# x2 closed by VectorE with its statistics right behind, the gate's halving folded in, two copies of ScalarE moved ahead

## The reference, cut to what matters

```python
h = relu(layernorm(x))
v = h @ W0                                   # 12 heads of 32
a = softmax(mask(leaky(src(tanh(v)) + dst(tanh(v)).T)))
gate = sigmoid(h @ H_w.T + H_b)
x2 = x + gate * elu(a @ v + b) + (1 - gate) * h
h1 = relu(layernorm(x2))
q, k, v1 = h1 @ Wq + bq, h1 @ Wk + bk, h1 @ Wv + bv
out = x2 + softmax(mask(q @ k.T / 8)) @ v1 @ Wf + bf
```

## Time and profile before

| what | value |
| --- | --- |
| timed runs, median of 3 | 1011.37 us (1010.96 to 1014.32) |
| profiled execution, its own time | 1006.25 us |
| its span | 1004.5 us |
| TensorE busy | 926.7 us, 92% |
| VectorE busy | 786.5 us, 78% |
| ScalarE busy | 641.2 us, 64% |
| GpSimd busy | 278.5 us, 28% |
| mean granted TensorE clock | 0.979 of full |

### The profile page before, as it was taken

The page is one execution under the profiler, slowest core; times in us unless marked ns, Lnnn a source line. Parts: engine busy times, 40 slices in busy tenths (PEclk is TensorE's granted clock), DMA queues, the critical chain, the costliest instruction groups (busy, mean ns, idle before and its releaser), DMA issues.

```text
span 1004.5 us, 24765 instructions
## 1 busy us (share of the span) xinstructions
PE 926.7 (92%) x9851; PEld 817.8 (81%) x9851; DVE 786.5 (78%) x1473; ACT 641.2 (64%) x1309; POOL 278.5 (28%) x337
## 2 busy tenths in 40 slices
PE   6599999999999999999999999999999999999595
PEld 5386888988888898888889888888988888898475
DVE  5877777879777787977778797777879777886804
ACT  5647658484865858486585848658584865857242
POOL 2224050331506033150603315060331506032210
PEclk9799999999999999999999999999999999999887
DMA  8303252231526223152522415252241525221102
GB/s 221 66 3 32 34 97 34 71 42 18 97 33 97 33 69 44 19 96 34 97 33 68 45 20 96 33 97 33 69 45 18 96 34 97 33 59 19 20 32 64
DMA packets 185077, 56.41 MB, mean 56 GB/s; under 512 B 166402, under 2 KB 184964, under 8 KB 184964
## 3 DMA queue, kind: packets, MB, share of 16 engines
q1 hardware_dynamic: 184964, 54.83, 31.2%
HBM read 17.07 MB, written 12.58 MB: 30 GB/s over the span
## 4 chain that ended last, share of the span: by engine, by line
PE 71%; DVE 22%; issue 2%; ACT 1%; SPq 1%; DMA 1%; POOL 0%; ACTq 0%; DVEq 0%; POOLq 0%
PE ps L694 12%; PE ps L696 12%; PE ps L695 12%; PE ps L761 8%; PE ps L765 7%; PE ps L762 7%; PE ps L680 5%; DVE p L1072 4%; DVE mx L1070 3%; DVE p L1044 3%; DVE x L1032 3%; PE ps L774 3%; DVE rs L1040 3%; PE ps L897 3%; PE ps L840 1%
## 5 line engine op out<-in xcount | busy, mean ns | idle before, releaser
L439 POOL TENSOR_TENSOR x_in<-x_in,ee 128x384 f32<-128x384 f32 x64 | 68.5, 1070 | 563.9 <-DVE ee L1057 563.9
L426 POOL TENSOR_TENSOR x_in<-x_in,bf_row 128x384 f32<-128x384 f32 x64 | 84.0, 1342 | 50.6 <-ACT p L459 50.6
L1070 DVE TENSOR_REDUCE mx<-ps 128x6 f32<-128x384 f32 x64 | 35.2, 550 | 75.8 <-PE ps L840 75.8
L1085 DVE COPY_PREDICATED_SCALAR z<-not_adj,masked 128x768 f32 x64 | 69.9, 1092 | 29.4 <-ACT z L550 29.4
L955 DVE TENSOR_TENSOR hT1l<-ps,hT1h 128x384 fp32r<-128x384 f32 x128 | 62.5, 549 | 26.0 <-ACT hT1h L464 26.0
L680 PE MATMUL ps<-ident,p 128*128 128x128 f32 x384 | 54.6, 287 | 26.9 <-DVE p L1044 15.5
L680 PEld LDWEIGHTS ps<-ident,p 128*128 128x128 f32 x384 | 44.6, 146 | 32.6 <-issue 18.3
L513 ACT ACTIVATE ps<-hb_all 128x384 f32<-128x384 f32 x56 | 27.6, 493 | 66.9 <-DVE x_in L1097 66.9
L531 ACT ACTIVATE QT<-ps,bq_col 128x512 f32<-128x512 f32 x48 | 33.0, 688 | 58.4 <-PE ps L765 58.4
L694 PE MATMUL ps<-Wf_hi,hT1h 128*128 128x384 f32 x192 | 67.6, 352 | 1.2 <-DVE x L1032 0.6
L432 POOL TENSOR_TENSOR x_in<-x_in,h 128x384 f32<-128x384 f32 x64 | 64.2, 1035 | 14.4 <-DVE Wf_lo L985 14.4
(11 more groups left out here) (134 smaller groups left out, 2815.7 us busy)
## 6 DMA issues: line engine op xcount, KB each, us to landing
x_in<-in_x_dram SPq DMA_DIRECT2D x16, 768.0 KB, 5.0
V<-v_tok SPq DMA_DIRECT2D x64, 192.0 KB, 5.8
V<-v_tok SPq DMA_DIRECT2D x128, 96.0 KB, 2.4
out_dram<-x_in SPq DMA_DIRECT2D x16, 768.0 KB, 3.5
x<-in_L_gnn_H_w_dram SPq DMA_DIRECT2D x1, 576.0 KB, 6.1
QT<-in_L_gnn_W_dram SPq DMA_DIRECT2D x3, 192.0 KB, 6.9
thT<-in_L_gnn_Wq_dram SPq DMA_DIRECT2D x1, 576.0 KB, 5.5
z<-in_L_gnn_Wk_dram SPq DMA_DIRECT2D x1, 576.0 KB, 6.5
```

Source lines behind the costliest of these rows:

```text
L426: pool.tensor_tensor(x_in[:, j % 3, t], x_in[:, j % 3, t], bf_row[:], ALU.add).then_inc(x2_biased, 1)
L439: pool.tensor_tensor(x_in[:, i % 3, t], x_in[:, i % 3, t], ee[:, t], ALU.subtract).then_inc(x2_made, 1)
L1070: dve.tensor_reduce(mx1[:, q], bank.rearrange("p (h m) -> p h m", m=N), AX_X, ALU.max).then_inc(max1_made, 1)
L1085: dve.copy_predicated(zu, not_adj[:, tiles].unsqueeze(2).broadcast_to((P, 2, PAIRS0, N)), masked0[:].unsqueeze(2).unsqueeze(3).broadcast_t ...
```

## The change

VectorE, in place of GpSimd, makes x2: `close(t)` gets a fourth instruction, x_in = -0.5 * ee + x_in, and the statistics of that tile follow it at once, each waiting for the one before. The gate stays g = tanh(z/2): ScalarE's four instructions that formed (1 + g) / 2 are gone, the third instruction of `close` multiplies by (g + 1), and the halving is the -0.5 of the fourth. The 1 that was added to h - ee goes into the second instruction. ScalarE's copies of the last two blocks of turned probabilities stand ahead of `exp1(2)` and `exp1(3)` now.

```diff
             # GpSimd
-                if real(i):
-                    pool.wait_ge(x_plus_h, TILES * (i + 1))
-                    for t in range(TILES):
-                        pool.wait_ge(gated, TILES * i + t + 1)
-                        pool.tensor_tensor(x_in[:, i % 3, t], x_in[:, i % 3, t], ee[:, t], ALU.subtract).then_inc(x2_made, 1)
             # ScalarE
-                if real(i):
-                    for t in range(TILES):
-                        act.wait_ge(gate_tanh, TILES * i + t + 1)
-                        act.activation(gate[:, t], gate[:, t], ACT.Identity, scale=0.5, bias=half[:]).then_inc(gate_made, 1)
...
-                exp1(2)
-                exp1(3)
                 if real(i):
                     for q in range(4, 6):
                         act.wait_ge(probs0_turned, 6 * i + q + 1)
                         act.activation(thT[:, q - 3], ps[:, job("probs0T_copied", q) % BANKS], ACT.Copy).then_inc(probs0T_copied, 1)
+                exp1(2)
+                exp1(3)
             # VectorE, close(t)
                         dve.wait_ge(elu_made, n)
+                        dve.scalar_tensor_tensor(x1[:, t], h0[:, par, t], 1.0, ee[:, t], ALU.add, ALU.subtract).then_inc(h_less_elu, 1)
+                        dve.wait_ge(h_less_elu, n)
+                        dve.wait_ge(gate_tanh, n)
+                        dve.scalar_tensor_tensor(ee[:, t], gate[:, t], 1.0, x1[:, t], ALU.add, ALU.mult).then_inc(gated, 1)
+                        dve.wait_ge(gated, n)
                         dve.wait_ge(x_plus_h, n)
-                        dve.tensor_tensor(x1[:, t], h0[:, par, t], ee[:, t], ALU.subtract).then_inc(h_less_elu, 1)
-                        dve.wait_ge(h_less_elu, n)
-                        dve.wait_ge(gate_made, n)
-                        dve.scalar_tensor_tensor(ee[:, t], x1[:, t], 1.0, gate[:, t], ALU.add, ALU.mult).then_inc(gated, 1)
-
-                def stats_of_x2(t):
-                    if real(i):
-                        dve.wait_ge(x2_made, TILES * i + t + 1)
+                        dve.scalar_tensor_tensor(x_in[:, i % 3, t], ee[:, t], -0.5, x_in[:, i % 3, t], ALU.mult, ALU.add).then_inc(x2_made, 1)
+                        dve.wait_ge(x2_made, n)
                         row_stats(1, x_in[:, i % 3, t], t, i)
...
                 close(3)
-                stats_of_x2(0)
-                stats_of_x2(1)
                 add_out(2)
                 values0(i + 1, 2)
-                stats_of_x2(2)
-                stats_of_x2(3)
```

## The result

| | before | after |
| --- | --- | --- |
| timed runs, median | 1011.43 us (1010.96 to 1014.32, 4 runs) | 1025.64 us (1024.86 to 1026.73, 4 runs) |
| ratio of the runs, 95% interval | | 1.0135 (1.0114 to 1.0156) |
| profiled execution, span | 1004.5 us | 1023.1 us |
| VectorE busy | 786.5 us | 807.3 us |
| ScalarE busy | 641.2 us | 612.5 us |

The change makes the kernel slower, by 14.2 us in the medians and by 18.6 us in the two profiled spans. The forecast was 17.0 more (1028.4, within 1020 to 1036).

What follows compares the result with a forecast made beforehand. TensorE, busy 92%, was taken to bound the kernel, with VectorE holding it up behind the scores. Stalls of 14.6 us plus 1.4 and 1.0 at the ends made 17.0; 1011.37 + 17.0 = 1028.4 us, range 1020 to 1036.

Steps and rivals of the forecast that it cites:

- The chain of the closing: On VectorE, four distances of 0.59 us plus a 0.465 statistic make a closing 2.825 instead of 1.66.
- What GpSimd's x2 had cost VectorE: Two closing instructions slowed while GpSimd made x2; with GpSimd idle, 0.70 + 0.58 = 1.28 us come back per body.
- The bank: `add_out(2)`, 2.45 us later, frees gate tile 2's bank too late: TensorE stalls 1.04 us in 14 bodies, 14.6 us.
- The slack of 1.54: `add_out(2)` ended at 483.57 and could end as late as 485.11 without delaying TensorE at gate tile 2.
- The other deadlines: Behind the first stall, h1 (slack 0.6 us) is in time by 0.1, and gate tile 3 has no second wait.
- ScalarE: Dropping four halvings, 2.1 us a body, and copying sooner gain nothing: ScalarE waits for TensorE, and VectorE's chain holds behind the scores.
- The rival in which the exponentials come late: Behind the scores, moved copies delay the exponentials, so `divide1(1)` waits in 15 bodies: 7.5 us on top, 1036; chance 0.09.
- The ends: In the first and last group TensorE waits for h1, so later `row_sums` counts directly: +1.4 and +1.0 us.
- The rule on semaphores: Semaphores between chained VectorE instructions cost nothing, so closing distances are 0.48: rival of 1012.4 us, chance 0.06; forecast used 0.59.

Runs made afterwards that it cites:

- the statistics back where they stood: The change with x2's four statistics at their earlier places, two behind the last closing, two behind values0 of tile 2: 1014.35 us, ratio 1.0073.
- `add_out(2)` sooner: The change with `add_out(2)` moved one closing earlier, right behind `add_out(1)`: 1021.58 us against 1008.12, ratio 1.0140.
- The pairs: The change with closings of two tiles interleaved, and `add_out(1)`, `add_out(2)` and the values at other places: 1006.23 us against 1008.24, ratio 0.9979.
- the second comparison: The unedited change timed again beside the kernel before, on another chip than at first: 1025.18 us against 1007.83, ratio 1.0183.
- ScalarE's part alone: The change with x2 by GpSimd again, statistics at their earlier places, halving left out, sooner copies kept: 1008.66 us against 1008.12, ratio 1.0006.
- the pairs with the two moves: Interleaved closings, plus next body's mask at the body's end and `divide0(3)` between attention 1's second and third low parts: 1002.39 us, ratio 0.9940.

## Why the prediction was right

**The chain of the closing.** A closing was foreseen at 2.825 us and measures 2.84. The distance between waiting neighbours was foreseen at 0.59 and measures 0.58 to 0.60 in four places of each closing. The instruction that was not in the trace takes 0.56, with 0.60 to the next. What GpSimd's x2 had cost VectorE went away as foreseen: no closing instruction is over 0.56. The Trainium skill ("SBUF — State Buffer", section "🔬 SBUF: two separate sides") says that VectorE with two SBUF inputs and a GpSimd instruction that reads SBUF take the shared ports as an exclusive lock, each for the whole instruction. The traces here agree. VectorE's long instructions of 1.25 to 1.26 and 1.13 us are there in the kernel before and with x2 by GpSimd again, each has two SBUF inputs and starts while GpSimd's x2 runs, and none is there in the change.

**The bank.** `add_out(2)` was to come 2.45 later and comes 2.50; the stall was to be 1.04 and is 1.07 at the tile and 1.06 in the body (59.67 less 58.61). It stands 14 times among TensorE's waits, as foreseen. The slack of 1.54 is bracketed: 0.90 and 1.09 of delay cost nothing at that tile, 2.50 costs 1.07.

**The other deadlines.** h1 was to be in time by 0.1 in the change, because the first stall delays TensorE too, and no wait for it shows. It does show once the first stall is taken away, in two kernels, and makes the projections about 0.2 us late in each.

The larger part of what those two kernels lose is at gate tile 3: 0.22 of 0.42 us a body, and 0.75 of 0.92. The prediction asked whether tile 3 would wait in the change, and was right that it would not, but it did not read the slack of that bank. Rows of the kernel before give it, on VectorE, ScalarE and TensorE:

```profile
485.15 0.52 DVE L1097 TENSOR_TENSOR x_in<-ps,x_in 128x384 f32<-128x384 f32 x1
...
486.28 0.49 ACT L513 ACTIVATE ps<-hb_all 128x384 f32<-128x384 f32 x1
...
487.26 0.33 PE L694 MATMUL ps<-Hw_hi,hT0h 128*128 128x384 f32 x1
```

`add_out(3)` ends at 485.67 and, by the same reading as for tile 2, could end as late as 486.67 (487.26 - 0.50 - 0.09): a slack of 1.00 us, less than tile 2's. With the statistics back where they stood it comes 1.10 later, with `add_out(2)` sooner 1.60 later, and both wait. In the change it comes 1.58 later, but TensorE is 1.07 late by then, so only 0.51 of the slack is used.

**ScalarE.** Its part is worth nothing, in both kernels that take its parts alone or away, and the reason is the one given: the 0.5 us that TensorE saves it waits for `divide1` later. The rival in which the exponentials come late can be read off the change itself, on ScalarE and VectorE:

```profile
468.32 0.97 ACT L566 ACTIVATE p<-p 128x384 f32<-128x384 f32 x2
...
469.83 0.94 DVE L1031 TENSOR_REDUCE rs<-p 128x12 f32<-128x768 f32 x1
```

The last two exponentials end at 469.29 and `divide1(1)` starts at 469.83: 0.54 us to spare, where 0.5 was foreseen.

**The ends.** The prediction had +1.4 at the first group and +1.0 at the last. TensorE's wait at the turning of h1 in the first group and in the last answers to the earlier trace rows:

```profile
79.08 2.98 PE L671 MATMUL ps<-ident,p 128*128 128x128 f32 x12 [1.29 <-ACT p L454]
...
972.86 2.79 PE L671 MATMUL ps<-ident,p 128*128 128x128 f32 x12 [10.93 <-ACT p L454]
```

The first comes 1.68 later, of which 0.3 was there ahead of the closings (the first of them starts at 63.04 instead of 62.72); the last wait is 10.93 instead of 9.88, 1.05 more.

**The rule on semaphores.** The Trainium skill ("VectorE: DVE Perf Modes", section "The DRAIN you can't avoid") measured eight copies and found that a semaphore after each costs nothing extra. For the instructions of this case a wait for the one right ahead does cost: 0.59 against 0.47 in one and the same operation and shape. The measurement decides. The pairs keep every wait of the change and run at 0.47, so it is not the semaphore as such that costs, but having to wait for the instruction right ahead. What the 0.12 us is made of was not tried. The pairs took the ratio from 1.0183 to 0.9979, about 19 us; `add_out(2)` sooner alone gave 4.

**The size.** The prediction had 17.0 us; the second comparison gives 17.4 and the first 14.2. The terms add up to it: 14 x 1.07 + 1.36 + 1.05 = 17.4. The forecast time, 1028.4, is 2.8 above the measured 1025.64, because the 17.0 were put on a median of the kernel before that came out some 3 us lower in every later comparison. What made that kernel slower in the first comparison is open: its spans body by body were not recorded in the timed runs.

## What to carry to other kernels

An engine that is not the bound still has deadlines. Read the slack of every one at the place, by the last moment at which the next engine could start and not be late, and sum what a change adds ahead of each: here 2.45 us against 1.54. Taking the worst stall away uncovers the next: behind it lay one of 1.00 us and one of 0.6. A saving on an engine that waits on both sides was worth nothing here, and a stall on VectorE that lies inside the slack is no reason to move work there. When work must go to VectorE, alternate two independent chains before giving it up: the same instructions took 0.47 instead of 0.59 us each, and together with `add_out` and `values0` at other places that turned a loss of 1.8% into a gain of 0.2%.

## What I had not expected

**TensorE's clock in the last body.** The profiled span grew by 18.6 us, 1.75 of it behind the last stall. Windows of 5 us from 0.7 us behind the first projection of the last body (length, busy of the five engines, granted clock, DMA): of the kernel before, of the change, of the kernel with ScalarE's part alone and of the pairs.

```profile
960.00:965.00 5.00, 5.00 (x23) 4.02 (x22) 0.00 (x0) 1.38 (x2) 1.51 (x2) 1.00 0.00 0
```

```profile
977.00:982.00 5.00, 5.00 (x17) 3.92 (x16) 0.00 (x0) 0.69 (x1) 1.47 (x2) 0.66 0.00 0
982.00:987.00 5.00, 5.00 (x23) 4.05 (x22) 0.00 (x0) 1.47 (x3) 0.00 (x0) 1.00 0.01 3
```

```profile
959.09:964.09 5.00, 5.00 (x15) 3.94 (x14) 0.00 (x0) 0.69 (x1) 1.49 (x2) 0.56 0.00 0
...
956.76:961.76 5.00, 5.00 (x16) 3.93 (x15) 0.00 (x0) 0.69 (x1) 1.50 (x2) 0.61 0.00 0
```

In the profile of the kernel before the clock was at its upper level (2.4 GHz) in this window. In the change it was at 0.66 on average, between that and the lower level (1.2 GHz), and from the first projection to the turning of probabilities TensorE took 29.12 instead of 27.37 us. Ahead of it TensorE had done nothing for 9.88 and 10.93 us, but the length of that pause is not the cause. ScalarE's part alone has a pause of 9.87 and a clock of 0.56, the pairs one of 8.93 and 0.61. Of the eleven traces of this study ten have 0.50 to 0.69 there, and only the one of the kernel before has 1.00. So the 1.75 us belongs to that one execution and not to the change, and it is part of why the two profiled spans differ by more than 17.4. What sets the clock apart in it is open.

**Two paces of the same matmuls.** In the last kernel the bodies of 58.42 us have no wait that those of 58.06 lack. TensorE over four matmuls of the output product, the first and the last shown, in a body of the short kind, and in one of the long kind:

```profile
181.01 0.33 PE L687 MATMUL ps<-Wf_hi,hT1l 128*128 128x384 f32 x1
...
181.53 0.34 PE L687 MATMUL ps<-Wf_hi,hT1l 128*128 128x384 f32 x1
```

```profile
297.08 0.34 PE L687 MATMUL ps<-Wf_hi,hT1l 128*128 128x384 f32 x1
...
297.61 0.34 PE L687 MATMUL ps<-Wf_hi,hT1l 128*128 128x384 f32 x1
```

The three distances take 0.52 us in the one and 0.53 in the other, that is 0.173 and 0.177 each, with a granted clock of 1.00 in both. From the first matmul of the output product to the turning of tanh(v) the first of these bodies takes 18.81 us (175.38 to 194.19) and the second 19.16 (291.87 to 311.03). That is the whole 0.35 us. The kernel with the statistics ahead of `add_out(2)` has three bodies of 58.92 among those of 58.60. It limits what a difference under 0.3% between two such kernels means. In the profiled execution of the pairs with the two moves the nine long bodies make 3.2 us (9 x 0.35), about what that kernel took over its forecast. Why the same products run at two paces is open.
